# An attention stage on one Trainium2 core: ScalarE's order of work per tile is changed, and the "one" of the softmax is summed with the exponents

## The reference

```python
def softmax_one(x, axis):
    x = x - jnp.max(x, axis=axis, keepdims=True)
    ex = jnp.exp(x)
    return ex / (1.0 + jnp.sum(ex, axis=axis, keepdims=True))
q = (x @ Wq.T + bq).reshape(S, B, HEADS, D_K)      # called with S=4, B=2048: the attention runs
k = (x @ Wk.T + bk).reshape(S, B, HEADS, D_K)      # over 4 positions, for each of 2048 rows
v = (x @ Wv.T + bv).reshape(S, B, HEADS, D_K)      # and 16 heads of 16 numbers
scores = jnp.einsum('ibhd,jbhd->ijbh', q, k) / np.sqrt(D_K)
scores = jnp.where(causal, scores, -jnp.inf)
attn = softmax_one(scores, axis=1)
out = jnp.einsum('ijbh,jbhd->ibhd', attn, v)
logits = xt @ wg                                    # the experts' router, from the same normalised rows
```

## Time and profile before

| what | value |
|---|---|
| time, median of 3 runs | 1402.9 us (1401.94 to 1403.82) |
| the profiled execution: its own time | 1404.15 us |
| the profiled execution: its span | 1402.3 us |
| busy in the span | PE 1167.3, DVE 1028.8, ACT 629.6, POOL 626.1 us |
| the attention stage | from about 263 us to about 557 us |
| one tile in its middle (406.81 to 423.74 us) | PE busy 14.62, DVE 14.91, ACT 6.62, POOL 13.05 us of 16.93; granted TensorE clock 1.00 |

### The profile page before, as it was taken

The page is one execution under the profiler, slowest core; times in us unless marked ns, Lnnn a source line. Parts: engine busy times, 40 slices in busy tenths (PEclk is TensorE's granted clock), DMA queues, the critical chain, the costliest instruction groups (busy, mean ns, idle before and its releaser), DMA issues. The chain is left out here.

```text
span 1402.3 us, 22325 instructions
## 1 busy us (share of the span) xinstructions
PE 1167.3 (83%) x7451; PEld 792.2 (56%) x7451; DVE 1028.8 (73%) x1972; ACT 629.6 (45%) x960; POOL 626.1 (45%) x538
## 2 busy tenths in 40 slices
PE   4799999588888884237999989999899998999910
PEld 3565565366666663124666656666566665666610
DVE  6767777659888889975777667776677666777638
ACT  4865555233333442004453544635446354463522
POOL 5600000038777777114464454644545445464430
PEclk9999999799999998558999999999999999999965
DMA  8270000001111112006455454554645545555469
GB/s 334 67 235 1 1 0 1 16 31 32 32 32 31 32 32 76 0 20 133 93 111 113 63 119 95 109 110 65 134 82 105 110 68 113 95 110 105 67 172 349
DMA packets 148958, 122.51 MB, mean 87 GB/s; under 512 B 88400, under 2 KB 133328, under 8 KB 148720
## 3 DMA queue, kind: packets, MB, share of 16 engines
q1 hardware_dynamic: 114912, 83.90, 20.1%
q0 software_dynamic: 25200, 35.85, 16.7%
q10 hardware_dynamic: 8736, 1.33, 0.5%
HBM read 58.91 MB, written 44.30 MB: 74 GB/s over the span
## 5 line engine op out<-in xcount | busy, mean ns | idle before, releaser
L1744 ACT ACTIVATE e_h_all<-e_pH,e_b1c,e_h_scale 128x512 f32<-128x512 f32 x256 | 199.8, 780 | 274.8 <-PE e_pH L1785 274.7
L1528 POOL DMA_INDIRECT e_xg<-xn_rows,e_icol x140 | 161.1, 1151 | 302.2 <-DVE e_icol L1560 269.4
L1799 PE MATMUL e_pY<-e_w_hi,e_h_hi 128*128 128x256 f16 x1024 | 279.6, 273 | 10.7 <-DVE e_w_lo L1619 10.7
L1801 PE MATMUL e_pY<-e_w_hi,late 128*128 128x256 f16 x1024 | 279.1, 273 | 0.0
L1800 PE MATMUL e_pY<-e_w_lo,e_h_hi 128*128 128x256 f16 x1024 | 279.1, 273 | 0.0
L1662 DVE TENSOR_TENSOR late<-e_h_all,e_h_hi 128x512 f16<-128x512 f32 x256 | 177.7, 694 | 97.0 <-ACT e_h_hi L1744 91.4
L1543 POOL DMA_INDIRECT expert_sums<-late,e_dcol x128 | 211.5, 1652 | 54.5 <-issue 35.8
L1783 PE MATMUL e_pH<-e_xT,e_w_hi 128*128 128x512 f16 x512 | 195.8, 382 | 23.4 <-DMA e_xT<-e_xs 15.5
L1785 PE MATMUL e_pH<-e_xT,e_w_lo 128*128 128x512 f16 x512 | 195.6, 382 | 0.0
L1784 PE MATMUL e_pH<-e_xT,e_w_hi 128*128 128x512 f16 x512 | 195.6, 382 | 0.0
L1799 PEld LDWEIGHTS e_pY<-e_w_hi,e_h_hi 128*128 128x128 f16 x1024 | 100.1, 98 | 34.6 <-DVE late L1662 16.1
(11 more groups left out here) (251 smaller groups left out, 2158.9 us busy)
## 6 DMA issues: line engine op xcount, KB each, us to landing
shared<-expert_w SPq DMA_DIRECT2D x18, 1024.0 KB, 8.0
expert_sums<-a_zero SPq DMA_DIRECT2D x10, 1024.0 KB, 11.3
x_st<-x SPq DMA_DIRECT2D x16, 512.0 KB, 9.3
xn_rows<-shared SPq DMA_DIRECT2D x16, 512.0 KB, 3.0
f_ya<-expert_sums SPq DMA_DIRECT2D x16, 512.0 KB, 7.5
out<-x_st SPq DMA_DIRECT2D x8, 1024.0 KB, 8.5
e_xg<-xn_rows,e_icol POOLq DMA_INDIRECT x140
e_xT<-e_xs SPq DMA_TRANSPOSE x136
```

The source lines that it names most:

```text
L1528: pool.indirect_dma_start(xg[:, q, 0:D + E], None, v.xn3_dram, bass.IndirectOffsetOnAxis(icol[u][:, q:q + 1], axis=0), bounds_check=N - 1, ...
L1744: last = act.activation(dst, pH[h % NPH][:, :], ACT.Relu, bias=b1c[eu][:, h:h + 1], scale=h_scale[eu][:, 0:1])
L1799: pe.matmul(pY[:, q, :], h_hi[:, h, cols], w2_hi[:, h, :], start=(h == 0), stop=False)
L1801: last = pe.matmul(pY[:, q, :], h_lo[:, h, cols], w2_hi[:, h, :], start=False, stop=(h == HT - 1))
```

## The change

Three things are edited. First, ScalarE's order: the turned logits of a tile (`put_logits`) are taken before the next queries instead of at the start of the next tile; and the keys of tile t + 1 are taken behind the exponents of tile t instead of ahead of them. Second, `ex` gets a fifth row that is filled with ones at the start; the exponents are written to rows 0 to 3 and the sum runs over five rows, so that the separate addition of one is gone. Third, the constant `zero16` has no tile of its own any more but lies in `d_found`, which is written only behind its last use.

```diff
-        ex = sb("c_ex", [P, B, B, H])
+        ex = sb("c_ex", [P, B + 1, B, H])
...
-        zero16 = sb("d_zero16", [P, P], BF16)
+        zero16 = found[:, 0:P // 2].bitcast(BF16)
...
-        SM = 6
+        SM = 5
...
                 dve.memset(sc[:, :, :, :], -1e30).then_inc(masked, 1)
+                dve.memset(ex[:, B:, :, :], 1.0).then_inc(masked, 1)
...
                     dve.tensor_reduce(mx[:, :], ex[:, :, :, :].rearrange("p j i h -> p (i h) j"), AX.X,
                                       ALU.add).then_inc(sm, 1)
                     dve.wait_ge(sm, SM * t + 4)
-                    dve.tensor_scalar(mx[:, :], mx[:, :], 1.0, None, ALU.add).then_inc(sm, 1)
-                    dve.wait_ge(sm, SM * t + 5)
                     dve.reciprocal(mx[:, :], mx[:, :]).then_inc(sm, 1)
...
-                take_qk(0, 0, reused=False)
+                take_q(0, reused=False)
+                take_k(0)
                 take_logits(0)
                 take_v(0, 0, reused=False)
                 take(xnT, pT, t_done, t_evac, 1)
-                take_qk(1, 1)
+                put_logits(0)
+                take_q(1)
 
                 def body(i, u, left):
+
                     t = 2 * i + u
-                    put_logits(t)
-                    act.wait_ge(ex_in, t + 1)
-                    act.activation(ex[:, :, :, :], ex[:, :, :, :], ACT.Exp).then_inc(ex_out, 1)
+                    exponents(t)
+                    if left >= 1:
+                        take_k(t + 1)
                     store_logits(t)
                     if left >= 2:
                         normalise(t + 2, u, i + 1)
...
                     if left >= 2:
                         take(xnT, pT, t_done, t_evac, t + 2)
-                        take_qk(t + 2, u)
+                    if left >= 1:
+                        put_logits(t + 1)
+                    if left >= 2:
+                        take_q(t + 2)
```

More of the change, by code:

```diff
@@ L999, in body @@
                         pool.memset(within2[:, :, :], 1.0).then_inc(filled, 1)
-                        pool.memset(zero16[:, :], 0.0).then_inc(consts_ready, 1)
+                        pool.memset(zero16, 0.0).then_inc(consts_ready, 1)
                         pool.tensor_copy(ident16[:, :], ident).then_inc(consts_ready, 1)
@@ L1073, in _ @@
                 dve.wait_ge(bias_ready, 5)
-                dve.wait_ge(masked, 3)
+                dve.wait_ge(masked, 4)
                 for n in range(3):
@@ L1102, in body @@
                     dve.wait_ge(sm, SM * t + 3)
-                    dve.tensor_tensor(ex[:, :, :, :].rearrange("p j i h -> p j (i h)"),
+                    dve.tensor_tensor(ex[:, 0:B, :, :].rearrange("p j i h -> p j (i h)"),
                                       sc[:, :, :, :].rearrange("p j i h -> p j (i h)"), spread(mx[:, :], B),
@@ L1115, in body @@
                     dve.tensor_tensor(att[u][:, :, :, :].rearrange("p j i h -> p j (i h)"),
-                                      ex[:, :, :, :].rearrange("p j i h -> p j (i h)"), spread(mx[:, :], B),
+                                      ex[:, 0:B, :, :].rearrange("p j i h -> p j (i h)"), spread(mx[:, :], B),
                                       ALU.mult).then_inc(att_ready, 1)
@@ L1260, in take, with take_q @@
                     act.activation(dst[:, :, :], src[:, :, :], ACT.Copy, scale=scale).then_inc(evac, 1)
-                def take_qk(t, u, reused=True):
+                def take_q(t, reused=True):
                     if reused:
@@ L1265, in take_qk, with take_k, exponents @@
                     take(q, pY, q_done, q_evac, t, scale=DK ** -0.5)
+                def take_k(t):
                     take(k, pX, k_done, k_evac, t)
+                def exponents(t):
+                    act.wait_ge(ex_in, t + 1)
+                    act.activation(ex[:, 0:B, :, :], ex[:, 0:B, :, :], ACT.Exp).then_inc(ex_out, 1)
                 def take_v(t, u, reused=True):
@@ L1368, in _ @@
                     if n == 0:
-                        pe.matmul(ptab, ident16[:, :], zero16[:, :], start=True, stop=False, skip_group_check=True)
+                        pe.matmul(ptab, ident16[:, :], zero16, start=True, stop=False, skip_group_check=True)
                     for a in range(WIDE):
@@ L1374, in _ @@
                     last.then_inc(used[n % 2], 1)
-                pe.matmul(ptab, ident16[:, :], zero16[:, :], start=False, stop=True,
+                pe.matmul(ptab, ident16[:, :], zero16, start=False, stop=True,
                           skip_group_check=True).then_inc(table, 1)
```

## The result

The changed kernel takes **1391.2 us** (median of 4 runs, 1390.62 to 1391.92) against 1403.28 us (4 runs) of the kernel before beside it: ratio 0.9918, 95% interval 0.9905 to 0.9930, so 0.8% faster. The forecast was 1391.3. The profiled execution took 1390.86 us, its span is 1389.1 us (before: 1402.3).

A forecast was written before the change was run, and what follows sets the result against it. The prediction took a ring of waits on TensorE, with a needless wait for the logits' copy, to bound the attention stage. Rounds 8.6 plus tail 3.0 gave 11.6 us off the median of 1402.9: 1391.3 us, range 1389.8 to 1392.8.

The forecast's parts named there:

- TensorE's ring: Attention stage, one output product of layer 0 to the next: sets the tile's period, 16.93 us, falling to 16.27.
- The rounds: Attention tiles between layer 0's output products: 0.66 us less in each of 13, 8.6 us in all.
- Exponents before keys: ScalarE's order: exponents end 0.26 us before the keys need ScalarE even in the worst case, so TensorE loses nothing.
- VectorE's ring: Attention round of VectorE and GpSimd: 15.93 us (15.83 to 15.98) after the change, under TensorE's 16.27.
- L + 3.7: Worst-case end of L1045, held by GpSimd's second multiplication, counted in us from L, the start of L1042.
- its rival with 0.08: VectorE's round binds at 16.5 to 16.8 us by a longer sum or unseen GpSimd turn: 1395 to 1399; chance 0.08.
- Taking turns: VectorE instructions with two SBUF inputs wait for the whole GpSimd instruction under way, and the reverse.
- The flat rival: L1045's 1.92 and the products' 4.12 us stay whatever GpSimd's phase; ring 16.47 us, 1393.7 us; chance 0.13.
- Fifth row: VectorE's sum grows by 0.1 us, the 0.20 us addition goes; worth 0.1 us only at the end.
- Tail: From the last output product to the end of the attention stage's sum: 3.0 us less, between 2.4 and 3.4.
- nothing changes: Rival: the releasers named are not the true ones, or a later stage gives time back; 1401 to 1404; chance 0.04.
- slower: Rival: products alternate with GpSimd's large instructions, 7.66 instead of 4.12 us, late subtraction holds up TensorE; 1430 us; chance 0.03.

The follow-up runs named there:

- logits_only: Changed kernel, but with the key copy ahead of the exponents as before; turned logits stay ahead of the queries: 1393.00 us, ratio 0.9931 to the kernel before.
- exponents_only: Changed kernel, but with the turned logits behind the keys again; exponents stay ahead of the keys: 1400.53 us, ratio 0.9981 to the kernel before.
- pad_small: Changed kernel plus one unused ScalarE copy of 128 numbers between exponents and keys of tiles 0 to 14: 1392.31 us, ratio 0.9920 to the kernel before.
- pad_large: Changed kernel plus two unused ScalarE copies of 512 numbers between exponents and keys of tiles 0 to 14: 1395.77 us, ratio 0.9942 to the kernel before.
- values_norm: Changed kernel with the value product ahead of layer 0's output product and, on ScalarE, the normalisation ahead of the exponents: 1389.41 us, ratio 0.9901 to the kernel before.

## Why the prediction was right

*What bounds it.* TensorE's ring, with the logits' copy as the only needless wait in it. logits_only has the whole gain of the rounds without the exponents' move, exponents_only has none of it.

*The rounds.* 16.27 us was forecast and 16.27 measured, apart from the one longer round; 1.08 us from key copy to output product became 1.07. 13 x 0.66 = 8.6 us against 8.9 between the last output products (508.42 and 499.51), of which 0.3 are from ahead of the first changed round.

*Exponents before keys.* Free by a cover put at 0.26 us or more. In the changed kernel it is 1.07 us at first and never under 0.30; pad_small leaves 0.12 of it and keeps the round; pad_large shows that it ends. How far the cover reaches exactly was not measured.

*VectorE's ring.* Here the prediction was wrong in a term and still right in the total. It put the end of the subtraction at 13.60 us after GpSimd's start "whatever `layer0`'s start is within some tenths", and from that VectorE's ring at 15.93 us, safely under 16.27. 13.60 holds where GpSimd's first multiplication is the one that L1046 waits for (before, logits_only, values_norm). In the changed kernel the move of the exponents starts GpSimd 0.66 to 1.45 us ahead of L1043, its second multiplication is first in nine tiles of thirteen, and the subtraction ends 14.15 us after GpSimd's start: a loop of 16.45 to 16.50 us, over TensorE's. The prediction had this turn in its bound for the keys (L + 3.7; measured 406.75 - 403.05 = 3.70) but not in VectorE's ring, and its rival with 0.08, a turn that makes VectorE's round bind at 16.5 to 16.8, is what these nine tiles show. It does not bind in the changed kernel because the turns change hands before the cover is used up. It does in pad_large, at 16.47.

*Taking turns.* The flat rival is out: L1046 takes 1.22 or 2.44 us according to which engine was first, the round is 16.27, and values_norm goes down to 15.94. That pad_large has the flat rival's 16.47 is a coincidence of sums.

*Fifth row.* The sum's growth was put at 0.1 us and is 0.11 in the row shown (0.70 us; 0.74 at most). It is hidden in the rounds, as said.

*Tail.* 3.6 us against 3.0, and outside the 2.4 to 3.4 that were allowed for. The prediction left open whether GpSimd would start just ahead of the last products and took the middle of 3.4 and 2.4; it did not in the changed kernel, and it did in pad_small. What that costs was put at 1.0 us; 0.85 was measured on the products.

*The total.* 11.6 forecast; 12.1 between the medians of the same runs, 12.2 in the stage. That 1391.3 meets 1391.2 so closely is partly luck: the gain was 0.5 us larger, and the kernel before measured 1403.28 this time instead of 1402.9. The other figure given, 1392.6 for a profiled execution, was 1.7 us too high (1390.86): about 0.6 from the tail, 0.3 from ahead of the first changed round, 0.7 from behind the stage, where nothing was changed. The rivals "nothing changes" and "slower" had no part: the products took 3.00 or 4.12 us in every tile but the last two, and the later stages gave nothing back.

## What to carry to other kernels

An idle engine with a named releaser is not yet the bound: close each ring (what must happen before the same instruction runs again, and over how many tiles) and compare the sums; the two waits here stood side by side, and only one was in the longest ring. In an in-order list a copy whose input is there and whose target is free can be late only because of what stands ahead of it, so look for instructions whose input was ready long before, and move them into the idle time that lies earlier; then ask what the moved wait now stands in front of. After 0.7 us a tile the next ring was 0.3 us behind, and reaching it took changes on two engines. Where two engines take turns at something, a ring has no one length: this one was 15.94 or 16.47 us, by who came first. So read the idle time ahead of the critical instruction over several tiles; if it shrinks from tile to tile, another ring is already longer.

## What the runs showed of the hardware that was not expected

Two products on 64 rows of the array each ran side by side: 1.06 us for both, and 1.05 us for one when the other had started 0.5 us earlier. Splitting a wait between them bought nothing.

Which of VectorE and GpSimd is first by 0.07 us decides which of them waits: 1.22 and 2.51 us, or 2.44 and 1.50, for the same two instructions. The loop of the two engines is 15.94 us a tile where L1046 waits for the tail of GpSimd's first multiplication, and 16.47 where the second one is ahead of it (values_norm and pad_large). Over four VectorE products that alternate with GpSimd's large instructions, being 0.07 us behind instead of 0.16 us ahead made 8.52 of 7.67 us.
